# Transposes of the next batch before the second half of A times V: one reordering on two engines

## The reference

```
mod = (silu(c) @ wmod) -> sa, ca, ga, sb, cb, gb          # per batch, 256 wide
h   = layernorm(x) * (1 + ca) + sa
q, k, v = givens(h, r0), givens(h, r1), givens(h, r2)     # rotation of feature pairs
A   = softmax((2 + 2 q.k) / scale + bias)                 # 512 x 512, one head
u   = A v ;  x1 = x + ga * u / sqrt(|u|^2)
h2  = layernorm(x1) * (1 + cb) + sb
out = x1 + gb * (shared FFN(h2) + 16 experts, each on its 64 best tokens per batch)
```

## Time and profile before

| | |
|---|---|
| three runs | 2358.26, 2363.18, 2363.24 us; median 2363.18 us |
| the profiled execution | 2360.59 us, its span 2358.7 us |
| TensorE busy | 2285.4 us, 97% of the span, 13676 matmuls |
| weight loads | 2002.7 us (85%) |
| VectorE, GpSimd, ScalarE busy | 63%, 61%, 51% |
| granted TensorE clock, mean | 0.992 of full speed |

### The profile page before, as it was taken

One profiled execution on the slowest core, in us unless ns is written; L12 is line 12 of the kernel. 1 busy time (PEld: TensorE's weight loads), 2 busy tenths in 40 slices (PEclk: granted clock), 3 DMA queues, 4 the chain that ended last, 5 costly groups with the idle time before them and its releaser, 6 DMA issues.

```text
span 2358.7 us, 40220 instructions
## 1 busy us (share of the span) xinstructions
PE 2285.4 (97%) x13676; PEld 2002.7 (85%) x13676; DVE 1483.5 (63%) x2823; ACT 1197.0 (51%) x2330; POOL 1436.2 (61%) x1351
## 2 busy tenths in 40 slices
PE   6999999999999999999989999999999999999997
PEld 4788888888888888888778888888888888888886
DVE  6676776877877777788575555545455555555543
ACT  4666676766766766666543333333333333333332
POOL 4466566566566566575545666666666666666664
PEclk8999999999999999999999999999999999999999
DMA  3121221221212212212244443444444444443433
GB/s 103 59 72 65 76 73 64 77 71 65 76 61 77 76 60 76 77 61 77 74 108 81 90 86 60 89 83 88 90 81 62 87 86 88 89 84 59 88 60 45
DMA packets 82967, 179.37 MB, mean 76 GB/s; under 512 B 12240, under 2 KB 47216, under 8 KB 82832
## 3 DMA queue, kind: packets, MB, share of 16 engines
q0 software_dynamic: 49152, 67.14, 17.9%
q1 hardware_dynamic: 33680, 110.27, 14.0%
HBM read 110.03 MB, written 67.34 MB: 75 GB/s over the span
## 4 chain that ended last, share of the span: by engine, by line
PE 54%; DVE 1%; POOL 1%; issue 1%; DMA 1%; ACT 1%; SPq 0%; DVEq 0%; POOLq 0%
PE ps L370 17%; PE ps L371 17%; PE ps L372 17%; PE ps L522 2%; DMA stage<-in_wd 1%; PE ps L437 0%; PE ps L480 0%; POOL out L1381 0%; POOL x_rows L1319 0%; PE ps L473 0%; PE ps L463 0%; DVE hidden_f L964 0%; DVE hidden_f L1221 0%; ACT gelu L704 0%; PE ps L412 0%
## 5 line engine op out<-in xcount | busy, mean ns | idle before, releaser
L370 PE MATMUL ps<-x_t,weights 128*128 128x512 f32 x1536 | 614.4, 400 | 14.0 <-issue 4.6
L1381 POOL DMA_INDIRECT out<-x_rows,step_token x256 | 418.5, 1635 | 320.7 <-DVE x_rows L1200 261.9
L371 PE MATMUL ps<-x_t,weights 128*128 128x512 f32 x1536 | 601.7, 392 | 0.0
L372 PE MATMUL ps<-x_t,weights 128*128 128x512 f32 x1536 | 600.7, 391 | 0.0
L370 PE MATMUL ps<-weights,hidden 128*128 128x256 f32 x2048 | 585.0, 286 | 9.4 <-POOL hidden L1281 5.8
L371 PE MATMUL ps<-weights,hidden 128*128 128x256 f32 x2048 | 581.8, 284 | 0.0
L372 PE MATMUL ps<-weights,hidden 128*128 128x256 f32 x2048 | 581.8, 284 | 0.0
L812 ACT ACTIVATE gelu<-ps 128x512 f32<-128x512 f32 x256 | 152.8, 597 | 538.7 <-PE ps L372 538.7
L1221 DVE TENSOR_TENSOR hidden_f<-gelu,ps 128x512 f32<-128x512 f32 x256 | 175.6, 686 | 382.0 <-ACT gelu L812 381.9
L370 PEld LDWEIGHTS ps<-weights,hidden 128*128 128x128 f32 x2048 | 394.6, 193 | 18.8 <-issue 7.1
L371 PEld LDWEIGHTS ps<-weights,hidden 128*128 128x128 f32 x2048 | 394.7, 193 | 7.3
(11 more groups left out here) (179 smaller groups left out, 3633.8 us busy)
## 6 DMA issues: line engine op xcount, KB each, us to landing
mod_b<-mod_rows SPq DMA_DIRECT2D x32, 640.0 KB, 5.2
x_rows<-in_x SPq DMA_DIRECT2D x32, 512.0 KB, 3.5
h_rows<-stage SPq DMA_DIRECT2D x32, 512.0 KB, 2.9
out<-y_rows SPq DMA_DIRECT2D x32, 512.0 KB, 2.6
stage<-in_wg SPq DMA_DIRECT2D x16, 512.0 KB, 3.6
stage<-in_wd SPq DMA_DIRECT2D x16, 512.0 KB, 5.9
stage<-in_wu SPq DMA_DIRECT2D x16, 512.0 KB, 4.8
sa_ca_b<-mod_rows SPq DMA_DIRECT2D x31, 256.0 KB, 4.7
```

Source lines behind the costliest of these rows:

```text
L370: pe.matmul(o, lhs(HI), rhs(HI), start=start, stop=False)
L371: pe.matmul(o, lhs(HI), rhs(LO), start=False, stop=False)
L372: return pe.matmul(o, lhs(LO), rhs(HI), start=False, stop=stop)
L1381: pool.indirect_dma_start(out=out_rows, out_offset=bass.IndirectOffsetOnAxis(ap=ICUR[g][:, t:t + 1], axis=0), in_=X1[:, g % 2, t * D:(t + ...
```

## The change

Two neighbours swap places in TensorE's list and two in ScalarE's. On TensorE `x_transposes(i+1)` stands in front of `a_times_v(i, 1)`; on ScalarE `h1_high(i+1)` stands in front of `squares(i, (2, 3))`. No instruction, wait, DMA or buffer is added or taken away, and the lists of VectorE, GpSimd and SyncE stay as they are. In pass 0 and in passes 1 to 30 both swaps apply; pass 31 has no next batch.

```diff
@@ -568,10 +568,10 @@   (TensorE)
                     a_times_v(i, 0)
                 if valid(i - 1):
                     gate_up(i - 1, 1)
-                if valid(i):
-                    a_times_v(i, 1)
                 if valid(i + 1):
                     x_transposes(i + 1)
+                if valid(i):
+                    a_times_v(i, 1)
                 if finish is not None:
                     top_transposes(finish)
                 if start is not None:
@@ -783,10 +783,10 @@   (ScalarE)
                     squares(i, (0, 1))
                 if valid(i - 1):
                     hidden(i - 1, 1)
-                if valid(i):
-                    squares(i, (2, 3))
                 if valid(i + 1):
                     h1_high(i + 1)
+                if valid(i):
+                    squares(i, (2, 3))
                 if valid(i - 1):
                     hidden(i - 1, 2)
```

More of the change, by code:

```diff
@@ L570, in iteration @@
                     gate_up(i - 1, 1)
+                if valid(i + 1):
+                    x_transposes(i + 1)
                 if valid(i):
                     a_times_v(i, 1)
-                if valid(i + 1):
-                    x_transposes(i + 1)
                 if finish is not None:
@@ L785, in iteration @@
                     hidden(i - 1, 1)
+                if valid(i + 1):
+                    h1_high(i + 1)
                 if valid(i):
                     squares(i, (2, 3))
-                if valid(i + 1):
-                    h1_high(i + 1)
                 if valid(i - 1):
```

## The result

| | before | after |
|---|---|---|
| median | 2362.72 us (2358.26 to 2363.24, 4 runs) | 2401.03 us (2399.09 to 2405.93, 4 runs) |
| ratio | 1 | 1.0172, 95% interval 1.0154 to 1.0190 |
| profiled execution, span | 2360.59, 2358.7 us | 2405.93, 2404.1 us |
| granted TensorE clock | 0.992 | 0.992 |

The account below looks back on a forecast made before the run. TensorE, busy 97% of the span, bounds the kernel. Waits 33.9, restart 3.2, passes 18 and 26 2.3, pass 10 0.5 and pass 0 2.35 make 42.3 on 2360.6: 2403 us, 8-in-10 range 2388 to 2421.

Parts of the forecast that it names:

- The wait in an ordinary pass: In twenty passes the transposes wait about 1.20 us on TensorE for `ln1_apply`, 23.9 us in all.
- the restart: TensorE's start behind the wait for `ln1_apply`: 0.12 us a pass in 27 passes, 3.2 us.
- The 1.35 us of wait in four passes: Four of the seven passes (3 to 8 and 19) where `ln1_apply` starts later: the transposes wait 1.35 us.
- The two feeders: GpSimd's multiplication and VectorE's `attention_out(i, 0)`, two operations of 0.68 us, both end where `ln1_apply` starts.
- It comes back in every pass: The chain hangs on TensorE at both ends, so lateness in one pass delays the next by as much.
- Passes 18 and 26: Transposes already wait there; `attention_out(i, 1)` and TensorE's restart behind the score rows move 1.15 us later, 2.3 us for both.
- Pass 10: Pass with a short score-row wait (1.52 us): cost between 0 and 1.32 us, taken as 0.5.
- Pass 0: No FFN work to hide anything: `attention_out(0, 1)` starts 2.35 us later, counted whole.
- Rival 1, the clock: TensorE's clock falls in the new waits: 2453 us if in every pass, 2420 if in one of three; 8%.
- Rival 2, no effect: TensorE works on matmuls behind the waiting transposes, so A times V fills the wait: 2361 us; 4%.
- Rival 3, faster: Earlier `h1_high` and `h1_low` free VectorE for quarter 2's product, up to 0.2 us a pass: 2354 us; 3%.

Follow-up runs that it names:

- the dose: One more VectorE operation ahead of `attention_out(i, 0)`: on the kernel before 2362.92 us (ratio 1.0018), on the changed kernel 2421.4 us (ratio 1.0264).
- the restart experiment: Changed kernel with `x_transposes` waiting for `at_hi` and `at_lo` first and `h1r_ready` last: 2404.19 us, ratio 1.0188.

## Why the prediction was right

It forecast 2403 us by 42.3 us more in passes 0 to 30; the median is 2401.03, the profiled passes took 42.4 us more. The mechanism is the one that was forecast: an uncovered wait for `ln1_apply` in each pass. That the sum is right to 0.1 us is luck, since terms that were off cancel: the loop passes gave 2.2 us more than forecast and passes 0, 18 and 26 0.4 more, pass 27 gave 1.5 less, pass 1 0.7 less and the other passes outside the loops 0.4 less. Step by step:

- **The wait in an ordinary pass.** Forecast 1.20 plus 0.12 of restart in twenty passes; the row of pass 22 has 1.27 idle, that of pass 30 1.08. Passes outside TensorE's loops became 1.23 to 1.29 us longer, near the forecast (1.32), but for 1 and 27. Those in the loops took about 0.1 us more than forecast (1.39 to 1.51 where 1.32 stood, 1.54 to 1.65 and 1.78 to 1.81 where 1.47 and 1.65 stood), since the restart is 0.24 there and not 0.06. So the restart was mis-sized in 18 passes, 2 us in all; the row of pass 18 that it was taken from is one outside the loops. The 1.35 us of wait in four passes stands on no row shown; the trace of before has 1.34 to 1.36 there.
- **The two feeders.** The prediction let both end where `ln1_apply` starts, with two operations of 0.68 us on VectorE. They follow each other by 0.60, and GpSimd comes last by some 0.2 us, as the dose shows. The forecast does not hang on this, since it took the end of `ln1_apply` from its row.
- **It comes back in every pass.** Right: 31 waits. That the chain hangs on TensorE at both ends is what the dose shows: the 0.41 us by which it moved the end of the chain are 0.41 us of idle time in pass 22, and the ordinary passes became 0.20 to 0.48 us longer. Shortening the chain gives time back in the same way.
- **Passes 18 and 26.** Forecast restart of the next pass 1.15 us later; pass 18 became 1.26 us longer. The wait behind it shrank from 2.90 to 1.34 (about 1.5 forecast). Pass 10: 0.5 forecast, 0.51 measured, which is luck: 0.5 was picked between 0 and 1.32 without a sum. Pass 18 after:

```profile
713.74 1.09 PE L412 MATMUL ps<-consts,stage 128*128 128x128 f32 x8 [2.73 <-DVE stage L952]
...
722.44 0.47 PE L370 MATMUL ps<-x_t,rot_k 128*128 128x512 f32 x1 [1.34 <-DVE score_rows L1054]
```

- **Pass 0.** Forecast 2.35 us; measured 2.5, by another way, and so by luck. The 3.65 us wait of the transposes was followed by 5.6 us at half clock (PEclk, third number from the end; the others are length, and busy PE, PEld, DVE, ACT, POOL), in which the transposes and A times V took twice as long. Pass 1 added 0.66 instead of an ordinary 1.32: its idle time grew by 2.5 us (6.50 to 9.02), but its busy time fell by 1.9 (32.17 to 30.31) at a mean granted clock of 0.91 instead of 0.87.

```profile
47.58:53.19 5.61, 5.61 (x27) 5.61 (x28) 1.29 (x2) 1.07 (x2) 1.27 (x1) 0.50 0.00 0
```

- **Rival 1, the clock.** It did not come in ordinary passes: pass 22 ran at 1.00 behind its wait. At the turn of pass 26 the wait for the score rows is 1.25 us where it was 2.79, and the clock stayed at 1.00 behind it (0.50 before); pass 27 became 0.22 us shorter instead of 1.3 longer, which gave back some 1.5 us and hid the 2 us of the restart in the sum. The new long waits of the transposes, 2.73 and 2.72 us in passes 18 and 26, left the clock at 1.00 as well, but in the restart experiment it fell behind both (2.82 and 2.84 us), and with TensorE's swap alone too (2.72 and 2.74). So the forecast was in luck there as well. The windows are of the kernel after, behind the wait of pass 18 and at the turn of pass 26, and then of the restart experiment, passes 18 and 26:

```profile
714.00:722.44 8.44, 7.10 (x51) 6.29 (x49) 4.99 (x12) 3.18 (x8) 6.78 (x5) 1.00 0.15 62
...
1019.28:1022.50 3.22, 3.22 (x14) 2.67 (x15) 1.80 (x3) 2.67 (x6) 1.63 (x3) 1.00 0.00 0
```

```profile
712.00:716.00 4.00, 3.95 (x21) 3.98 (x22) 1.79 (x3) 1.69 (x3) 3.96 (x3) 0.57 0.19 76
...
1009.40:1012.80 3.40, 3.13 (x15) 3.16 (x16) 1.25 (x3) 1.69 (x3) 3.14 (x2) 0.51 0.02 5
```

- **Rival 2, no effect.** Wrong: with `gate_up(i-1, 1)` issued and the operands of A times V long there (they were multiplied at this very point before), TensorE stood still behind the waiting transposes. This is the row that was missing before; it agrees with what the Trainium skill, "TensorE: Matmul & The Clock Gate", section "Part 2: What happens when you issue a matmul", says of program order.
- **Rival 3, faster.** Its 0.2 us a pass were not there to be had: with ScalarE's swap alone, and with the transposes between the tiles, the weight loads wait for the product of quarter 2 just as long (6.2 us in 13 waits in both). The gelu holds that product: in pass 22 of the kernel before it ends at 833.76 + 0.60 = 834.36, and the product starts at 834.39 (timelines of ScalarE and VectorE).

```profile
833.76 0.60 ACT L704 ACTIVATE gelu<-ps 128x512 f32<-128x512 f32 x1 [1.61 <-PE ps L372]
...
834.39 0.69 DVE L964 TENSOR_TENSOR hidden_f<-gelu,ps 128x512 f32<-128x512 f32 x1
```

What was not tried: the chain shortened enough to let the changed order beat the kernel before.

## What to carry to other kernels

When a step moves forward on the engine that sets the time, read the time between the end of its input and its old start: that is all it can move before it waits, and the rest is paid in every pass, as the feeding chain starts from the same engine. An operation added to that chain costs only what it moves the chain's end by, so look which feeder comes last. If the step must go forward, move it by part of the block that covers it: 12 of 24 matmuls were enough here. Look at what else a long queue of small waits holds, too; the copies moved at the turn of a group were worth as much as the best place of the transposes (0.14 and 0.13%).

## What the runs showed of the hardware

The order of the three semaphore waits in front of the transposes changed how fast they start behind the last to come. With the late one first and two long-fulfilled ones behind it the start came 0.24 us after the input inside a loop and 0.05 outside; with the late one last 0.06 inside and 0.15 outside.

Two VectorE operations of 0.68 us on 128x512 f32 follow each other by 0.60 to 0.61 (833.58 to 834.19 in the run with ScalarE's swap alone), so a chain of them is shorter than the sum of its rows.

Whether the clock falls in a wait of near 3 us differed between executions of nearly the same order of work: behind 2.72 us in pass 26 it stayed in the kernel after, behind 2.74 it fell with TensorE's swap alone. The wait of 1.27 us in pass 22 left it at 1.00.
